# Four graph layers on one core: the relation layer gathers node features with their gates and applies the relation weights per unit of nodes, with no table per relation

## The chip, the core and the metric

The program runs on one core of a Trainium2 chip. The metric is the device time of one execution in microseconds (us), median of the runs. TensorE is called PE below, VectorE DVE, ScalarE ACT, GpSimd POOL, SyncE SP.

## What is computed

There are 6250 nodes with 128 features each and 106250 edges, sorted by destination: 17 per node on average, the node's own loop among them. Four layers follow one another, and each ends in a residual and a layer norm without weights. The third is the one that is changed:

```python
xw = einsum('ni,rio->rno', h, W)              # 8 relations
msg = xw[rel, src] + bias_term[rel]
gate = sigmoid(sum(msg * gw[rel], -1) + gate_bias[rel])
agg = segment_sum(msg * gate[:, None], dst)
out = relu(agg + h @ loop_weight)
```

The first and the fourth layer are attention layers, the second an edge MLP with two layer norms. Every one of them gathers one row per edge from a table of the nodes in HBM, and sums per destination.

## The kernel before, in words

Edges are worked through in 104 groups of 1024, 8 tiles of 128 edges each (`T` = 8, `NG` = 104). Nodes are 49 tiles of 128. They are finished in 13 units of 4 tiles (the last two of 3 and 2), once the groups that hold their edges are summed, so some 8.5 groups lie between one unit and the next. All time is spent in passes, one program per engine and pass, with a barrier of all engines between them: `first_tables`, `gat_pass(0)`, `mlp_pass`, `rel_pass`, `gat_pass(1)`. A check on the drawn edges picks between a fast and a slow path (`pick`, flag `fits`); the profile shows the fast one.

The order of the work is written out by hand. `drive` walks steps: in step n it emits the stages of a group (stage with lag k for group n - k) and then the pieces of units that are due (unit `at` + lag). Each engine runs its list in order and meets the others at semaphores.

`rel_pass` before. POOL issues 8 indirect DMAs per group (L1254, 831 in all), each of which fetches 128 rows of 128 floats from `rel_table`, which has a row for every node and relation, bias and gate already in it (50176 rows). The ring of row buffers is 8 groups deep: gather n waits until group n - 8 is summed. DVE builds the one-hot matrix `hot` of a group in one instruction (L1281, four buffers), PE multiplies rows by it, 8 products of 128 x 128 x 128 into one half-bank (L1411, two buffers `p_sum`), DVE adds the 128 columns to `acc` at the group's base, which it reads into a register first (`window`, L1287). In step n DVE does `one_hot(n)` and then `add(n-1)`, and PE's `add_up(n)` waits for `add(n-2)` only:

```python
pe.wait_ge(s.onehot, n + 1)
pe.wait_ge(s.gathered[n % RING], landed(sh, n))
wait(pe, s.added, n - 1)
```

A unit's `multiply` is 2 products a tile (L1427, L1428), then DVE's `residual` (L1294, L1295 and the moments L691 to L705), ACT's square root and scaling, transposes, the table product of the last layer (L1441) and its evacuation (L1316).

`mlp_pass` before. It gathers rows of 256 floats (L1593), adds the edge product (L1624), takes ACT's squares (L1789), scales and shifts them on DVE (L1630, L1632), gelu on ACT (L1799), sums on PE (L1889). The rows of `rel_table` are made behind the last sum, for all 49 tiles: two PE products of 512 columns a tile (L1954), DVE adds the bias for 1024 columns (L1746) and multiplies half of them by the gate (L1750), ACT the other half (L1855), SP stores 512 KB a tile. The row buffers and the PSUM banks of the groups are used for it, which is why it stands behind them. POOL clears `acc` when the last unit is multiplied (L1615, L1616).

## Time and profile before

| what | value |
|---|---|
| median of 3 runs | 4501.29 us (4498.23 to 4502.14) |
| span of the profiled execution | 5314.6 us, mean granted PE clock 0.674 |
| busy share of the span | PE 59%, DVE 47%, ACT 25%, POOL 60% |
| DMA | 567 MB, mean 107 GB/s |

The profiled execution gives its span only, and no time around it; it is 18% above the median of the runs, which are taken without the profiler. A row of the groups view gives busy time and mean ns of one instruction, then the idle time of the engine ahead of it and who ended it. Register loads, branches, waits and the issuing of DMAs don't count as busy and have no rows. An fp32 product on PE is two MATMUL instructions, so 8 products are 16 rows.

### The profile page before, as it was taken

To read this page: it belongs to the slowest core of one execution; us is meant where nothing else is said; L and a number is where in the kernel's file an instruction comes from. 1 tells how busy PE (TensorE), PEld (TensorE's weight loads), DVE (VectorE), ACT (ScalarE), POOL (GpSimd) and SP (SyncE) were. 2 spreads that over 40 slices of the span, in tenths; PEclk is the share of its full clock that TensorE was granted. 3 is DMA by queue.
4 is the path that set the end of the run, shared out by engine and by line. 5 is a ranking of instruction groups with operands and counts; after the bars stand their busy time and mean duration, and the time that the engine had idled before them with its cause. 6 is when DMAs were issued, how large, how long until landed. Compare 5 with 4: busy or idle time off the path is not lost. (4 is left out here: it accounts for less than half of the span.)

```text
span 5314.6 us, 52198 instructions
## 1 busy us (share of the span) xinstructions
PE 3112.7 (59%) x15416; PEld 2793.1 (53%) x15416; DVE 2515.0 (47%) x5316; ACT 1308.4 (25%) x3470; POOL 3165.2 (60%) x3335
## 2 busy tenths in 40 slices
PE   2666666666377787777871323333332666666666
PEld 2665666566366676666731223323231666666665
DVE  2344444445377878777870111112121454554555
ACT  0010010011267777777760000000000011111111
POOL 5666666663566666666206666666654666666662
PEclk6556556666689888988895566665665565555656
DMA  5444444443444444444241111111112333333331
GB/s 140 128 144 139 151 142 140 151 140 110 138 134 145 147 144 144 143 144 148 81 189 47 48 49 49 50 49 47 52 43 67 97 95 97 99 95 97 98 96 52
DMA packets 284107, 567.22 MB, mean 107 GB/s; under 512 B 108648, under 2 KB 157034, under 8 KB 283802
## 3 DMA queue, kind: packets, MB, share of 16 engines
q0 software_dynamic: 119664, 280.17, 20.3%
q1 hardware_dynamic: 157082, 278.92, 15.4%
q10 hardware_dynamic: 7056, 4.56, 0.3%
q8 instruction: 131, 2.15, 0.2%
q14 instruction: 174, 1.43, 0.1%
HBM read 465.83 MB, written 97.56 MB: 106 GB/s over the span
## 5 line engine op out<-in xcount | busy, mean ns | idle before, releaser
L840 POOL DMA_INDIRECT rows<-gat_table,src_i x1662 | 1568.6, 944 | 861.4 <-issue 464.9
L1593 POOL DMA_INDIRECT rows<-mlp_table,src_i x831 | 789.5, 950 | 527.0 <-issue 303.8
L1254 POOL DMA_INDIRECT rows<-rel_table,rel_i x831 | 783.9, 943 | 494.8 <-issue 343.4
L1129 PE MATMUL p_sum<-rows,hot 128*128 128x133 f32 x3328 | 781.6, 425 | 14.2 <-DVE rows L906 12.5
L1121 PEld LDWEIGHTS p_adc<-adw,hot_t 128*128 128x128 f32 x3328 | 688.1, 314 | 178.0 <-DVE hot_t L880 127.5
L1121 PE MATMUL p_adc<-adw,hot_t 128*128 128x8 f32 x3328 | 678.0, 342 | 147.7 <-DVE hot_t L880 108.4
L1129 PEld LDWEIGHTS p_sum<-rows,hot 128*128 128x128 f32 x3328 | 735.9, 326 | 17.2 <-DVE rows L906 15.6
L1411 PE MATMUL p_sum<-hot,rows 128*128 128x128 f32 x1664 | 324.5, 363 | 715.9 <-DVE hot L1281 365.9
L1411 PEld LDWEIGHTS p_sum<-hot,rows 128*128 128x128 f32 x1664 | 298.6, 272 | 744.3 <-DVE hot L1281 381.2
L1061 ACT COPY sums<-p_sum 128x133 f32<-128x133 f32 x208 | 56.4, 271 | 2211.6 <-DMA rel_index<-rel_i 1902.6
L1889 PE MATMUL p_sum<-hot,rows 128*128 128x128 f32 x3328 | 476.0, 310 | 201.8 <-ACT rows L1799 107.7
L1889 PEld LDWEIGHTS p_sum<-hot,rows 128*128 128x128 f32 x3328 | 461.3, 224 | 236.5 <-ACT rows L1799 123.5
L1136 PE MATMUL p_turn<-ident,sums 128*128 128x128 f32 x208 | 90.7, 436 | 781.1 <-ACT sums L1061 724.7
L906 DVE TENSOR_TENSOR rows<-rows,p_weight 128x1024 f32<-128x1024 f32 x208 | 253.7, 1220 | 610.5 <-ACT p_weight L1056 448.2
L1872 PE MATMUL p_pre<-w1e,eat 128*128 128x256 f32 x1664 | 436.8, 415 | 105.3 <-issue 104.4
L1136 PEld LDWEIGHTS p_turn<-ident,sums 128*128 128x128 f32 x208 | 35.5, 171 | 834.5 <-ACT sums L1061 772.8
L1287 DVE TENSOR_TENSOR acc_t<-acc_t,p_sum 128x128 f32 x104 | 29.8, 286 | 864.3 <-remote 775.9
L1872 PEld LDWEIGHTS p_pre<-w1e,eat 128*128 128x128 f32 x1664 | 337.3, 209 | 172.5 <-issue 123.3
L1789 ACT ACTIVATE junk<-rows 128x256 f32<-128x256 f32 x832 | 335.6, 404 | 294.5 <-DVE rows L1624 179.0
L1624 DVE TENSOR_TENSOR rows<-rows,p_pre 128x1024 f32<-128x1024 f32 x208 | 247.6, 1218 | 281.1 <-PE p_pre L1872 112.2
L1630 DVE SCALAR_TENSOR_TENSOR rows<-rows,stats,p_affine 128x256 f32<-128x256 f32 x832 | 335.1, 475 | 8.3
L886 DVE TENSOR_TENSOR z<-rows,p_adc 128x32 f32<-128x32 f32 x208 | 39.0, 188 | 561.1 <-remote 312.0
(239 smaller groups left out, 3693.9 us busy)
## 6 DMA issues: line engine op xcount, KB each, us to landing
drow<-in_dst_rows SPq DMA_DIRECT2D x208, 512.0 KB
hot_table<-hot SPq DMA_DIRECT2D x104, 512.0 KB
hot<-hot_table SPq DMA_DIRECT2D x104, 512.0 KB
rows<-gat_table,src_i POOLq DMA_INDIRECT x1662
rel_table<-rows SPq DMA_DIRECT2D x49, 512.0 KB, 2.6
eat<-in_edge_t SPq DMA_DIRECT2D x104, 128.0 KB
rows<-mlp_table,src_i POOLq DMA_INDIRECT x831
rows<-rel_table,rel_i POOLq DMA_INDIRECT x831
```

Source lines behind the costliest of these rows:

```text
L840: pool.indirect_dma_start(out=rows[:, n % RING, t, :], out_offset=None, in_=net.gat_table[:, :], in_offset=bass.IndirectOffsetOnAxis(ap=ne ...
L906: nc.vector.tensor_tensor(hr, hr, wt, ALU.mult).then_inc(s.messages, 1)
L1121: end = nc.tensor.matmul(p_adc[k][:, t, 0:2 * H], hot_t[:, k, t * P:(t + 1) * P], adw[:, half, :], start=True, stop=True)
L1129: end = nc.tensor.matmul(p_sum[:, 0:SUMS], hot[:, n % HALF, t, :], rows[:, n % RING, t, 0:SUMS], start=(t == 0), stop=(t == T - 1))
L1254: pool.indirect_dma_start(out=rows[:, n % RING, t, :], out_offset=None, in_=net.rel_table[:, :], in_offset=bass.IndirectOffsetOnAxis(ap=ne ...
L1411: end = nc.tensor.matmul(p_sum[n % 2][:, 0:P], rows[:, n % RING, t, :], hot[:, n % HALF, t, :], start=(t == 0), stop=(t == T - 1))
L1593: pool.indirect_dma_start(out=rows[:, n % RING, t, :], out_offset=None, in_=net.mlp_table[:, :], in_offset=bass.IndirectOffsetOnAxis(ap=ne ...
L1624: nc.vector.tensor_tensor(rows[:, slot, tt, :], rows[:, slot, tt, :], p_pre[half][:, :, :], ALU.add).then_inc(s.pre, 1)
L1630: nc.vector.scalar_tensor_tensor(rows[:, slot, t, :], rows[:, slot, t, :], stats[:, slot, 1, t:t + 1], p_affine[:, 0, :], ALU.mult, ALU.mult)
L1789: nc.scalar.activation(junk[:, t % (T // 2), :], rows[:, slot, t, :], ACT.Square, accum_out=stats[:, slot, 0, t:t + 1])
L1872: end = nc.tensor.matmul(p_pre[half][:, j, :], eat[:, ring, half, :], w1e[:, j, :], start=True, stop=True)
L1889: end = nc.tensor.matmul(p_sum[k][:, b, :], rows[:, n % RING, t, b * F:(b + 1) * F], hot[:, half, t, :], start=(t == 0), stop=(t == T - 1))
```

## The change

The relation layer is turned round: sum first, multiply after. The table `gated_table` has one row per node: 128 features plus one, and 8 gates (`GATED` = 136 floats). `mlp_pass` writes it unit by unit: DVE `lift` adds 1 to the features, PE transposes them and multiplies by `rel_gate` (8 columns), DVE adds the gate bias, ACT takes tanh, DVE turns that into the sigmoid. The bias of a relation is spread over its weights once (`lift_weights`), which the added 1 makes up for. 9 of the 13 units do this between groups, 4 (`late`) behind the last one; the last unit starts 4 steps after the one before it and not 6 (`LAST_APART`). POOL clears most of `acc` ahead of the last unit's product. The index of node and relation, its load of edge types in `first_tables`, and its store are gone.

In `rel_pass` the gathers read `gated_table` with the node's index. A group is cut into 4 pairs of tiles (`PAIRS`), each with 24 nodes x 8 relations = 192 columns (`KEYS`) from its own first destination. Per group DVE picks the edge's gate out of 8 (three small instructions), builds `hot` as 8 instructions of 192 columns (is the key equal, times gate), PE does 8 products with 192 columns into 4 sums, and DVE adds 4 pieces of 192 columns to a ring of 12 node tiles by 8 relations, each at a place that it reads into a register. PE's wait is now for `add(n-1)`, and DVE does `add` ahead of `one_hot`. `multiply` has 9 products a tile, one with the loop weight and 8 with the relation weights on every eighth column of the ring, and `residual` clears 1024 columns a tile. `prepare` works out keys and ring places once, ahead of the first group (some 17 DVE instructions on up to 832 columns). A second flag, `near`, worked out at the start of `gat_pass(0)`, picks the fast path of this pass: every edge of a pair within 24 nodes of its first, and the ring not overrun. The slow path is rewritten too (not shown).

```diff
+PAIRS = T // 2
+SPAN = 24
+KEYS = SPAN * R
+RING_TILES = 12
+GATED = F + R
...
+        self.ring = self.acc[:, :, :].rearrange("p a c -> p (a c)")
...
-        self.rel_table = dram("rel_table", (sh.NP * R, F))
-        self.rel_index = dram("rel_index", (P, sh.NG, T), I32)
+        self.gated_table = dram("gated_table", (sh.NP, GATED))
...
+        rows = s.sb("rows", [P, RING, T, GATED])
+        hot = s.sb("hot", [P, HALF, T, KEYS])
...
-        p_sum = [s.ps(f"p_sum{k}", [P, 512]) for k in range(2)]
-        p_iota = s.ps("p_iota", [P, P])
+        p_sum = [s.ps(f"p_sum{k}", [P, 2, 2 * P]) for k in range(2)]
+        p_keys = s.ps("p_keys", [P, KEYS])
...
-                        out=rows[:, n % RING, t, :], out_offset=None, in_=net.rel_table[:, :],
-                        in_offset=bass.IndirectOffsetOnAxis(ap=net.rel_i[:, n, t:t + 1], axis=0),
+                        out=rows[:, n % RING, t, :], out_offset=None, in_=net.gated_table[:, :],
+                        in_offset=bass.IndirectOffsetOnAxis(ap=net.src_i[:, n, t:t + 1], axis=0),
...
+            def gated(kinds, slot):
+                nc.vector.tensor_tensor(mask[:, :, :], tiled(kinds, T, R), over_tiles(p_keys[:, 0:R], T, R), ALU.is_equal)
+                dve.drain()
+                nc.vector.tensor_tensor(mask[:, :, :], mask[:, :, :], rows[:, slot, :, F:GATED], ALU.mult)
+                dve.drain()
             def one_hot(n):
+                dve.wait_ge(s.gathered[n % RING], landed(sh, n))
+                gated(types[:, n, :], n % RING)
+                nc.vector.tensor_reduce(gate[:, n % 2, :], mask[:, :, :], AX.X, ALU.add)
+                dve.drain()
                 wait(dve, s.summed, n - HALF + 1)
-                nc.vector.tensor_tensor(hot[:, n % HALF, :, :], tiled(net.reld[:, n, :], T, P), over_tiles(p_iota[:, :], T, P), ALU.is_equal).then_inc(s.onehot, 1)
+                for t in range(T):
+                    end = nc.vector.tensor_scalar(hot[:, n % HALF, t, :], p_keys[:, :], key[:, n, t:t + 1], gate[:, n % 2, t:t + 1], ALU.is_equal, ALU.mult)
+                end.then_inc(s.onehot, 1)
 
             def add(n):
-                first = window(dve, net, n)
                 dve.wait_ge(s.summed, n + 1)
-                part = net.acc[:, 0, bass.ds(first, P)]
-                nc.vector.tensor_tensor(part, part, p_sum[n % 2][:, 0:P], ALU.add)
-                dve.drain().then_inc(s.added, 1)
-            def residual(unit):
+                for w in range(PAIRS):
+                    v = n * PAIRS + w
+                    first = dve.value_load(ring_i[0:1, v:v + 1], min_val=0, max_val=MARGIN - R)
+                    part = net.ring[:, bass.ds(first, KEYS)]
+                    nc.vector.tensor_tensor(part, part, p_sum[w // 2][:, w % 2, 0:KEYS], ALU.add)
+                    end = dve.drain()
+                end.then_inc(s.added, 1)
+            def close(unit):
+                for t in range(unit.first, unit.first + unit.tiles):
+                    if t and t % RING_TILES == 0:
+                        nc.vector.tensor_tensor(net.ring[:, 0:KEYS], net.ring[:, 0:KEYS], net.ring[:, MARGIN:MARGIN + KEYS], ALU.add)
+                        dve.drain()
+                        nc.vector.memset(net.ring[:, MARGIN:MARGIN + KEYS], 0.0)
+                dve.drain().then_inc(s.closed, 1)
+            def residual(unit, fast):
 
                 m, tiles = unit.tiles, tiles_of(unit)
                 dve.wait_ge(s.node_product, unit.u + 1)
                 nc.vector.scalar_tensor_tensor(net.x[:, tiles, :], pu[:, 0:m, :], 0.0, net.x[:, tiles, :], ALU.max, ALU.add)
-                nc.vector.memset(net.acc[:, 0, columns(unit)], 0.0)
+                if fast:
+                    for t in range(unit.first, unit.first + m):
+                        nc.vector.memset(net.ring[:, ring_at(t) * R:(ring_at(t) + P) * R], 0.0)
+                else:
+                    nc.vector.memset(net.acc[:, 0, columns(unit)], 0.0)
...
-                drive(sh, [(one_hot, 0), (add, 1)], pieces)
+                drive(sh, [(add, 1), (one_hot, 0)], pieces(True))
...
-                pe.wait_ge(s.gathered[n % RING], landed(sh, n))
-                wait(pe, s.added, n - 1)
+                wait(pe, s.added, n)
                 for t in range(T):
-                    end = nc.tensor.matmul(p_sum[n % 2][:, 0:P], rows[:, n % RING, t, :], hot[:, n % HALF, t, :], start=(t == 0), stop=(t == T - 1))
+                    w = t * PAIRS // T
+                    end = nc.tensor.matmul(p_sum[w // 2][:, w % 2, 0:KEYS], rows[:, n % RING, t, 0:F], hot[:, n % HALF, t, :],
+                                           start=(t % (T // PAIRS) == 0), stop=(t % (T // PAIRS) == T // PAIRS - 1))
...
+                        pe.wait_ge(s.closed, unit.u + 1)
+                    else:
+                        pe.wait_ge(s.added, sh.NG * sh.NT)
+                    pe.wait_ge(s.xt_ready, unit.u + 1)
+                    wait(pe, s.variance, unit.u)
+                split = min(2, unit.tiles)
+                for t in (range(split), range(split, unit.tiles))[part]:
+                    nc.tensor.matmul(pu[:, t, :], xt[:, t, :], lw[:, :], start=True, stop=False)
+                    if fast:
+                        first = ring_at(unit.first + t)
+                        for r in range(R):
+                            end = nc.tensor.matmul(pu[:, t, :], by_relation[:, first:first + P, r], net.rel_w[:, r, :], start=False, stop=(r == R - 1))
...
-                for i in range(unit.tiles):
-                    t = unit.first + i
-                    sp.wait_ge(s.dve_scaled, t + 1)
-                    sp.wait_ge(s.act_scaled, t + 1)
-                    sp.dma_start(table[t:t + 1, :, :].rearrange("t p c -> p (t c)"), tab_of(unit, i).rearrange("p r f -> p (r f)")).then_inc(s.stored[unit.u % TABS], 16)
-            pieces = [(load_unit_weights, WEIGHTS_FIRST), (store_table, OfTable(1))]
+                sp.wait_ge(s.tab_done, unit.u + 1)
+                sp.dma_start(table[:, tiles_of(unit), :], stage[:, unit.u % 2, 0:unit.tiles, :]).then_inc(s.stored[unit.u % 2], 16)
+            pieces = [(load_unit_weights, WEIGHTS_FIRST), (store_table, OfTable(4 + HALF))]
...
-            def evacuate(unit, fast):
-                k = unit.u % 2
+                dve.drain().then_inc(s.outer_factored, 1)
+            def lift(unit):
+                m, k = unit.tiles, unit.u % 2
+                dve.wait_ge(s.normed, unit.u + 1)
+                wait(dve, s.stored[k], 16 * (unit.u // 2))
+                nc.vector.tensor_scalar(stage[:, k, 0:m, 0:F], net.x[:, tiles_of(unit), :], 1.0, None, ALU.add).then_inc(s.lifted, 1)
+            def gate_logits(unit):
+                m = unit.tiles
                 dve.wait_ge(s.gate_product, unit.u + 1)
-                wait(dve, s.gate_ready, unit.u)
-                nc.vector.tensor_tensor(logit[:, 0:unit.tiles, :], p_gate[:, 0:unit.tiles, :], over_tiles(net.rel_gate_bias[:, :], unit.tiles, R), ALU.add).then_inc(s.gate_logits, 1)
-                dve.wait_ge(s.summed, sums_done(fast))
-                wait(dve, s.stored[unit.u % TABS], 16 * kept_before(unit, TABS))
-                for i in range(unit.tiles):
-                    t = unit.first + i
-                    tab = tab_of(unit, i)
-                    dve.wait_ge(s.tab_product, t + 1)
-                    nc.vector.tensor_tensor(tab, p_tab[t % 2], net.rel_b[:, :, :], ALU.add).then_inc(s.tab_read, 1)
-                    dve.drain()
-                    if i == 0:
-                        dve.wait_ge(s.gate_ready, unit.u + 1)
-                    nc.vector.tensor_tensor(tab[:, 0:by_dve, :], tab[:, 0:by_dve, :], tiled(gate[:, k, i, 0:by_dve], by_dve, F), ALU.mult).then_inc(s.dve_scaled, 1)
-            def pieces(fast):
-                return steps + [(lambda unit: evacuate(unit, fast), OfTable(1))]
-            steps = [(copy_w2t, WEIGHTS_FIRST + 2), (fold_gates, WEIGHTS_FIRST + 3), (join, 6), (inner_factors, 8), (node_affine, 9), (residual, 11), (outer_factors, 13)]
+                nc.vector.tensor_tensor(logit[:, 0:m, :], p_gate(unit)[:, 0:m, :], over_tiles(net.rel_gate_bias[:, :], m, R), ALU.add).then_inc(s.gate_logits, 1)
+            def gates(unit):
+                m = unit.tiles
+                dve.wait_ge(s.curved, unit.u + 1)
+                nc.vector.tensor_scalar(stage[:, unit.u % 2, 0:m, F:GATED], curve[:, 0:m, :], 0.5, 0.5, ALU.mult, ALU.add)
+                dve.drain().then_inc(s.tab_done, 1)
+            steps = [(copy_w2t, WEIGHTS_FIRST + 2), (lambda unit: lift_weights(unit, 0), WEIGHTS_FIRST + 4), (lambda unit: lift_weights(unit, 1), WEIGHTS_FIRST + 5),
+                     (fold_gates, WEIGHTS_FIRST + 6), (join, 6), (inner_factors, 8), (node_affine, 9), (residual, 11), (outer_factors, 13),
+                     (lift, NORMED_AT), (gate_logits, OfTable(2)), (gates, OfTable(4))]
```

DVE in the relation pass, one steady step. Names: `combined_1` and `inner_turned_1` are printed for the semaphore `summed`, `stored2_1` for `gathered`; L663 and L1374 load a register; ISA rows are register work. Before:

```order
L1281 TENSOR_TENSOR hot<-reld_all,p_iota 128x1024 [waits combined_1]
L663 TENSOR_LOAD base_i
L663 ISA x2
L1287 ISA [waits combined_1]
L1287 TENSOR_TENSOR acc_t<-acc_t,p_sum_5 128x128
```

In the change:

```order
L1374 TENSOR_LOAD ring_i [waits inner_turned_1]
L1374 ISA x2
L1376 ISA
L1376 TENSOR_TENSOR acc_t<-acc_t,p_sum_5 128x192
L1374 TENSOR_LOAD ring_i
L1374 ISA x2
L1376 ISA
L1376 TENSOR_TENSOR acc_t<-acc_t,p_sum_5 128x192
...
L1354 TENSOR_TENSOR mask<-types,p_keys 128x64 [waits stored2_1]
L1356 TENSOR_TENSOR mask<-mask,rows 128x64
L1363 TENSOR_REDUCE gate<-mask 128x8
L1367 TENSOR_SCALAR hot<-p_keys,key,gate 128x192 [waits inner_turned_1]
L1367 TENSOR_SCALAR hot<-p_keys,key,gate 128x192 x7
```

The register load stood ahead of the wait for the sum and now stands behind it, four times, and everything that PE needs for the next group comes behind that.

PE at a unit of the relation pass, between two groups. Before:

```order
L1427 MATMUL pu_5<-ident,acc_t 128x128 [waits base_spread_1,folded_1]
L1428 MATMUL pu_5<-lw_5,xt_5 128x128
L1427 MATMUL pu_5<-ident,acc_t 128x128
L1428 MATMUL pu_5<-lw_5,xt_5 128x128
L1427 MATMUL pu_5<-ident,acc_t 128x128
L1428 MATMUL pu_5<-lw_5,xt_5 128x128
```

In the change:

```order
L1570 MATMUL pu<-lw,xt 128x128 [waits tab_done_1,product_1,base_ready_1]
L1574 MATMUL pu<-rel_w,acc_t 128x128 x8
L1570 MATMUL pu<-lw,xt 128x128
L1574 MATMUL pu<-rel_w,acc_t 128x128 x8
L1570 MATMUL pu<-lw,xt 128x128
```

Eight products of a unit became 36, in the same place between two groups.

## Rows read from the trace of the kernel before

**Rows 1.** Stages: us from the start, length, busy of each engine, PEclk, DMA share, GB/s

```profile
core 0: us, PE busy (x) PEld busy (x) DVE busy (x) ACT busy (x) POOL busy (x), PEclk, DMA share, GB/s
0.00:51.00 51.00, 23.71 (x159) 22.43 (x159) 23.73 (x76) 8.57 (x14) 11.86 (x8) 0.90 0.65 174
51.00:1260.00 1209.00, 760.66 (x3519) 707.58 (x3519) 539.25 (x1203) 97.26 (x370) 784.04 (x831) 0.60 0.48 141
1260.00:1339.00 79.00, 50.20 (x263) 43.03 (x262) 44.88 (x123) 13.45 (x40) 0.00 (x0) 0.69 0.19 66
1339.00:2576.00 1237.00, 910.99 (x5080) 801.26 (x5080) 909.59 (x1647) 843.82 (x2092) 789.52 (x831) 0.86 0.46 144
2576.00:2646.00 70.00, 57.51 (x343) 52.07 (x343) 56.31 (x114) 48.53 (x113) 0.00 (x0) 0.85 0.12 38
2646.00:2790.00 144.00, 116.42 (x365) 57.51 (x363) 105.13 (x172) 94.17 (x256) 10.80 (x2) 0.92 0.45 180
2790.00:3969.00 1179.00, 368.18 (x1914) 338.63 (x1914) 189.60 (x386) 38.30 (x82) 783.94 (x831) 0.61 0.19 49
3969.00:4025.00 56.00, 24.91 (x143) 22.53 (x142) 21.63 (x72) 9.31 (x21) 0.52 (x2) 0.65 0.07 15
4025.00:5230.00 1205.00, 752.73 (x3397) 705.04 (x3397) 571.73 (x1362) 136.11 (x431) 784.14 (x831) 0.58 0.36 96
5230.00:5314.60 84.60, 47.39 (x238) 42.99 (x237) 53.19 (x164) 18.87 (x51) 0.35 (x1) 0.63 0.07 22
```

**Rows 2.** The timeline of the relation pass: start, us, engine, line, idle before

```profile
2788.93 0.29 DVE L1336 COPY p_iota<-iota_row 128x128 f32<-128x128 f32 x1 [4.92 <-PEq L204]
2790.06 2.35 DVE L1281 TENSOR_TENSOR hot<-reld_all,p_iota 128x1024 f32<-128x1024 f32 x2 [0.83 <-issue]
2791.46 0.95 POOL L1254 DMA_INDIRECT rows<-rel_table,rel_i  x1 [0.30 <-issue]
2792.71 0.94 POOL L1254 DMA_INDIRECT rows<-rel_table,rel_i  x1 [0.30 <-issue]
...
3020.79 6.77 PE L1411 MATMUL p_sum<-hot,rows 128*128 128x128 f32 x32 [4.47 <-issue]
3021.05 0.16 DVE L714 TENSOR_TENSOR work<-scale 128x4 f32<-128x4 f32 x1
3021.30 0.16 DVE L716 SCALAR_TENSOR_TENSOR work<-work 128x4 f32<-128x4 f32 x1
...
3057.68 0.29 DVE L1287 TENSOR_TENSOR acc_t<-acc_t,p_sum 128x128 f32 x1 [2.43 <-PE p_sum L1411]
3058.09 1.22 DVE L1281 TENSOR_TENSOR hot<-reld_all,p_iota 128x1024 f32<-128x1024 f32 x1
```

**Rows 3.** Who waited for whom in the relation pass

```profile
DVE acc_t L1287 <- remote: 764.8, 45, 43.2
POOL rows L1254 <- remote: 150.5, 29, 10.7
```

**Rows 4.** Groups by shape on DVE: relation pass, then the first attention pass, then MLP

```profile
L1287 DVE TENSOR_TENSOR acc_t<-acc_t,p_sum 128x128 f32 x97 | 27.8, 286 | 847.8 <-remote 764.8 <-issue 50.6 <-PE p_sum L1411 32.5
...
L1294 DVE SCALAR_TENSOR_TENSOR x_nodes<-pu,x_nodes 128x512 f32<-128x512 f32 x10 | 6.9, 691 | 28.7 <-remote 28.1
...
L942 DVE MEMSET acc_t<- 128x1024 f32 x10 | 9.1, 912 | 1.6 <-issue 1.6
...
L892 DVE TENSOR_SCALAR z<-z 128x32 f32<-128x32 f32 x98 | 20.2, 206 | 7.9 <-issue 0.4
```

**Rows 5.** Timeline of the MLP pass, DVE: eight instructions of 256 columns, two pointers

```profile
2007.36 3.22 DVE L1630 SCALAR_TENSOR_TENSOR rows<-rows,stats,p_affine 128x256 f32<-128x256 f32 x8
```

**Rows 6.** Groups by shape in the stretch of the table, 2646 to 2790 us

```profile
L1954 PE MATMUL p_pre<-rel_w,hot 128*128 128x512 f32 x196 | 98.1, 647 | 8.8 <-DVE rows L1746 8.8
L1855 ACT ACTIVATE rows<-rows,gate 128x128 f32<-128x128 f32 x196 | 62.6, 390 | 37.3 <-DVE rows L1746 36.9
L1746 DVE TENSOR_TENSOR rows<-p_pre,rel_b 128x1024 f32<-128x1024 f32 x49 | 59.7, 1219 | 10.4 <-PE p_pre L1954 10.4
...
L1750 DVE TENSOR_TENSOR rows<-rows,gate 128x512 f32<-128x512 f32 x49 | 33.9, 692 | 8.9 <-ACT gate L1849 4.7
```

450 lines of the change are left out of this document (275 added, 175 removed).

## The prediction

> **What bounds the kernel now.** I read the stages first [rows 1]. Four stretches of 1179 to 1237 us hold 831 gathers each, 4830 of 5315 us; the other six add up to 484.6 us. In the four, POOL has the same 784 to 790 us of work, while PE ranges from 368 to 911 us and DVE from 190 to 910. What they share is the gather. The timeline shows its pace: one starts each 1.25 us, 0.94 us of work and 0.30 us in which nothing is waited for [rows 2]. 831 of these are 1039 us. The waits then show why the relation pass took 1179 us: POOL stood 151 us on a full ring of row buffers, and DVE waited 765 us in 45 pieces, 17 us each, for something the profile can't name [rows 3], far more than PE's work between them explains. While no gathers run, in the table stretch, DVE shows no such waits [rows 6]. The ring of 8 groups hides most of them.
>
> The profiled execution is 813 us longer than the median of 4501.3. If the 484.6 us outside the gathers cost the same in both, a gather costs (4501.3 - 484.6) / 3324 = 1.208 us in the timed runs, less than the unblocked 1.25 of the profile. So in the timed runs POOL is hardly blocked, and these waits are mostly the profiler's. I sum against the median: engine time is taken over from the rows one to one, the gather at 1.208. The relation pass then has 1004 us of gathers, 9.66 us a group. Against its own time the same sum would be 5315 plus the differences below, and more for the waits named under the rivals.
>
> **What goes.** The table stretch: 144 us in the profile, of which PE's products are 98 us and DVE's two instructions 94 us for 49 tiles [rows 6]. What stays behind the last sum is the chain of the last unit (two tiles) with three late units beside it. For that I take 35 us, an estimate from the 56 us stretch that ends the relation pass with its two last units [rows 1]; with less waiting in a timed run the stretch was 110 to 144 us, so 75 to 109 us go. I take **85 us**. POOL's two clears lay beside it and cost nothing before or after. The edge types, the index and its store were in the first 51 us, beside the node loads; 0 to 3 us, taken as 0, covered by the tables of that stage. The row fetched grows from 512 to 544 bytes with DMA at 0.19 busy: no cost. POOL issues the same 831 gathers.
>
> **What is added outside the relation pass.** DVE gets `lift`, the logits and the gates for 9 units in the MLP pass, some 1 us a unit, and ACT a tanh whose table may have to be loaded. DVE is 74% busy there, 8.7 us a group [rows 1], against 9.66 us of gathers, so little cover is left: **8 us**, bounds 0 and 25. The work for the flag at the start of `gat_pass(0)` is some 8 us on DVE while 8 groups of gathers run ahead, and DVE is 45% busy there: nothing.
>
> **What changes in the relation pass.** Before, DVE and PE had slack: `hot` was four buffers ahead and the sum had two. Now follow the new order. PE's group n needs `hot(n)`; DVE builds that behind `add(n-1)`; that waits for PE's group n-1. Nothing overlaps: a group costs DVE's adds, plus DVE's one-hot, plus PE's products. Piece by piece:
>
> - Adds. Before, one add with its drain took 0.41 us from start to start (57.68 to 58.09) [rows 2]; 64 more columns at one a cycle are 0.07. Each now has a register load in its way, behind the drain of the add before. No row shows a load. The gap of 0.83 us ahead of the first `hot` [rows 2] holds one load and a branch: upper bound 0.83, lower bound 0 (it could run under the add). I take three quarters of that gap, 0.62, since the drain stands between. 4 x (0.41 + 0.07 + 0.62) = **4.4 us**, bounds 1.9 and 5.2.
> - One-hot. Three small instructions with drains: those of 4 columns start 0.25 us apart [rows 2], of 32 columns they take 0.04 more [rows 4], so 0.28 each, 0.84. Then eight of 192 columns with two pointers each and a PSUM source. Nearest are the eight of 256 columns in 3.22 us [rows 5], 0.40 each, less 0.07 for 64 columns: 0.33 each, 2.65. Together **3.5 us**, bounds 2.8 and 3.8.
> - Products. 32 instructions of 128 columns took 6.77 us, 0.212 each [rows 2], at the lower of the two clock levels (1.2 GHz). 16 of 192 columns are 5.1 us there and half at 2.4 GHz. Stretches with PE about half busy or more between gathers show a mean granted clock of 0.58 to 0.61 [rows 1]; 2.55 / 0.6 = **4.25 us**, bounds 2.6 and 5.1.
> - Three hand-overs and the last product's way through: 0.4 us.
>
> The loop is 12.55 us, against 9.66 for the gathers. So the loop becomes the bound: 104 x 12.55 = 1305 us. On top, per unit: PE's 36 products are 72 instructions at 0.177 us (0.6 of the clock), 12.7 us, beside 7.9 us of DVE's adds and one-hot, so 4.8 us show. DVE's residual is 0.69 + 4 x 0.91 [rows 4] and some 1.6 us of moments, 5.9 us beside 4.65 us of PE, 1.3 us. 13 units: 80 us. `prepare` takes DVE some 11 us and its loads 3, beside the first 10 us of gathers: 4 us. The pass is 1389 us in place of 1004, **+385 us**.
>
> A register load has a price in the Trainium skill: DMA: Bandwidth & Descriptors, in the section on latency and other measured facts, gives about 600 ns as its floor. By that the sum would be 8 us lower; no row here shows it. The Trainium skill also speaks against where the keys lie: VectorE: DVE Perf Modes, Why PSUM operands drop a tier, says that an fp32 instruction with a PSUM operand runs at the plain rate, while one with a single SBUF source could run twice as fast. By that the eight instructions would lose 0.1 us each with keys in SBUF, 83 us over the pass; no row of this trace has such an instruction.
>
> **Sum.** 4501 + 385 - 85 + 8 = 4809, forecast **4810 us**.
>
> **Rivals.**
>
> 1. The loop still fits under the gathers. Then only the table's saving shows: 4501 - 85 + 8 = **4424 us**. It decides where the loop falls below 9.6 us, 3 us under my sum. For it: loads that hide (0 and not 0.62) give 2.5 us, full clock 1.7. Against it: both would have to come at once, and the pass before held the clock at 0.61 [rows 1]. Chance 0.09.
> 2. The waits of DVE [rows 3] are not only the profiler's. Before, a ring of 8 groups swallowed them; a loop that is itself the bound has no such cushion, and each wait lengthens it. Of 765 us at most 151 blocked POOL, so some 600 us are added: 4810 + 600 = **5410 us**. It decides as soon as waits of 17 us occur in timed runs. Against it is the 1.208 us. A weaker form of it is why my range reaches further up. Chance 0.08.
> 3. The change doesn't do what it says: the flag `near` falls, and the slow path runs. That has 49 x 8 x 8 products a group at 0.21 us or more, over 60 ms in all. With 17 edges per node 256 edges cover some 15 nodes, against 24 allowed, so 0.01.
> 4. Costs and saving cancel within 9 us: 0.02.
>
> My forecast has 0.80. **Range.** At the low ends together short of rival 1, a loop of 10.6 us and a saving of 105, the time is 4501 + (1102 + 40 - 1004) - 105 + 5 = 4539. At the high ends, a loop of 14.4 with 130 us for units, saving 75: 4501 + 624 - 75 + 10 = 5060, and some waits left. I give 4550 to 5120. Slower than before by over 0.2% (9 us, about what a measurement can tell from no change): forecast, rivals 2 and 3, 0.89; faster 0.09; the same 0.02.
>
> **What would show it.** In the changed kernel's profile POOL's gathers of the relation pass should be interrupted in every group, waiting for PE's last product, and the pass should be much longer than 1179 us. The adds should start 1.1 us apart, the eight one-hot instructions 0.33 us apart, and PE should start each group right behind the last of them, never behind a gather. The stretch between the last MLP gather and the first relation gather should shrink from 214 us to some 110 to 140. I am wrong if gathers run at 1.25 us without waits, if adds come 0.5 us apart, or if DVE's waits of 17 us fill the pass and the time is above 5120.

## The result, and the profile after

The changed kernel takes **4934.8 us** (median of 4 runs, 4932.7 to 4939.2) against 4500.3 (4498.2 to 4502.1) for the kernel before: **1.097 times as long, interval 1.095 to 1.098**, 435 us slower. The forecast was 4810 with a range of 4550 to 5120, so it held in sign and range and came out 125 us short.

The profiled execution of before that stands ahead of the prediction was a disturbed one: its span was 5314.6 us, 813 more than its runs. The same kernel, profiled again beside the experiments, has a span of 4503.3. Stages are therefore compared with that second profile. Here are its stages, in the columns of [rows 1]: the MLP pass, the stretch that makes the table of relations, the relation pass up to its last add, and what lies between that and the first gather of the last layer:

```profile
1126.50:2168.00 1041.50, 855.05 (x5243) 771.77 (x5244) 932.90 (x1701) 862.46 (x2154) 788.39 (x831) 0.93 0.55 173
2168.00:2348.50 180.50, 142.52 (x544) 81.77 (x543) 136.34 (x232) 119.26 (x308) 11.33 (x3) 0.92 0.37 148
2348.50:3392.00 1043.50, 439.23 (x2021) 414.26 (x2022) 204.72 (x417) 41.73 (x90) 783.97 (x831) 0.62 0.22 56
3392.00:3427.00 35.00, 9.26 (x37) 7.28 (x35) 9.67 (x42) 5.88 (x13) 0.48 (x1) 0.55 0.05 13
```

And the same four stretches of the changed kernel:

```profile
1122.00:2166.00 1044.00, 857.48 (x5292) 770.60 (x5293) 924.62 (x1691) 857.81 (x2144) 790.80 (x831) 0.93 0.57 174
2166.00:2256.00 90.00, 50.13 (x307) 44.93 (x305) 64.44 (x163) 56.18 (x118) 11.53 (x5) 0.78 0.09 27
2256.00:3802.00 1546.00, 686.31 (x2656) 660.97 (x2657) 637.83 (x1824) 41.76 (x90) 784.72 (x831) 0.69 0.17 40
3802.00:3855.40 53.40, 21.64 (x88) 19.74 (x87) 14.08 (x47) 5.89 (x13) 0.48 (x1) 0.64 0.04 9
```

POOL works 784 us in the relation pass both times. The pass is 1546.0 us now and was 1043.4, +502.6. The stretch ahead of it is 90.6 and was 181.0, -90.4. Behind the last add it is 53.5 and was 35.0, +18.5. The first stage with the first attention pass gives -4.4, the MLP pass +2.1, all the rest -0.8. That is +427.6, the difference of the two spans (4930.9 and 4503.3). Outside the relation pass and its two neighbours nothing moved.

The waits of the relation pass say who holds up whom. Columns: engine and what it waited for, us in all, times, the longest. These answer to [rows 3]:

```profile
PE p_sum L1549 <- DVE hot L1367: 866.4, 93, 25.8
...
DVE acc_t L1376 <- PE p_sum L1549: 493.2, 90, 5.9
POOL rows L1327 <- PE p_sum L1549: 418.3, 82, 9.1
...
DVE acc_t L1376 <- issue: 274.2, 326, 6.3
```

There are no waits of DVE on something unnamed any more. PE waits for the one-hots, DVE for PE's product, POOL for PE's product, in nearly every group. One group in the timeline, of DVE and PE, shows the circle; it answers to [rows 2]:

```profile
2379.16 0.22 DVE L1354 TENSOR_TENSOR mask<-types,p_keys 128x64 f32<-128x64 f32 x1
2379.46 0.23 DVE L1356 TENSOR_TENSOR mask<-mask,rows 128x64 f32<-128x64 f32 x1
2379.76 0.22 DVE L1363 TENSOR_REDUCE gate<-mask 128x8 f32<-128x64 f32 x1
2380.06 3.17 DVE L1367 TENSOR_SCALAR hot<-p_keys,key,gate 128x192 f32<-128x192 f32 x8
...
2383.29 4.82 PE L1549 MATMUL p_sum<-hot,rows 128*128 128x192 f32 x16 [8.73 <-DVE hot L1367]
...
2388.87 0.35 DVE L1376 TENSOR_TENSOR acc_t<-acc_t,p_sum 128x192 f32 x1 [5.63 <-PE p_sum L1549]
...
2389.99 0.36 DVE L1376 TENSOR_TENSOR acc_t<-acc_t,p_sum 128x192 f32 x1 [0.77 <-issue]
...
2391.12 0.35 DVE L1376 TENSOR_TENSOR acc_t<-acc_t,p_sum 128x192 f32 x1 [0.77 <-issue]
...
2392.25 0.35 DVE L1376 TENSOR_TENSOR acc_t<-acc_t,p_sum 128x192 f32 x1 [0.77 <-issue]
...
2392.72 0.22 DVE L1354 TENSOR_TENSOR mask<-types,p_keys 128x64 f32<-128x64 f32 x1
```

From mask to mask is 13.56 us: 0.90 for the mask and gate, 3.2 for eight one-hots, PE's first product 0.06 behind them, 4.82 of products, 0.76 to the first add, three more adds 1.13 apart, 0.47 to the next mask. In such a group DVE and PE never work at once. The granted clock of PE was 0.50 for the first 4.0 us of these products and 1.00 from 2387.3 us on, when they were nearly done. The 81 cycles away from the units are 13.73 us in the mean. In the 1.13 us from add to add only 0.35 are the add; the idle 0.77 in front of each holds a drain and a register load, which have no rows.

The groups by shape, up to 3370 us, which answer to [rows 4]:

```profile
L1367 DVE TENSOR_SCALAR hot<-p_keys,key,gate 128x192 f32<-128x192 f32 x600 | 238.0, 469 | 6.9 <-issue 1.2
L1376 DVE TENSOR_TENSOR acc_t<-acc_t,p_sum 128x192 f32 x296 | 104.9, 354 | 544.8 <-PE p_sum L1549 351.0 <-issue 193.7
```

### The profile page after: what moved, and what is told of

The parts are those of the page before. It is cut to its first block and busy times, and to the rows that moved or that the text cites. A ratio compares the mean times of both kernels' runs of the same rounds, so it can differ in the third digit from the quotient of the medians.

```text
span 4930.9 us, 56065 instructions
## 1 busy us (share of the span) xinstructions
PE 3180.4 (64%) x15914; PEld 2923.8 (59%) x15914; DVE 2866.6 (58%) x6664; ACT 1243.1 (25%) x3270; POOL 3169.7 (64%) x3336
## 3 DMA queue, kind: packets, MB, share of 16 engines
q1 hardware_dynamic: 156940, 256.65, 15.9%
## 5 line engine op out<-in xcount | busy, mean ns | idle before, releaser
L1327 POOL DMA_INDIRECT rows<-gated_table,src_i x831 | 784.8, 944 | 672.5 <-PE p_sum L1549 418.3
L1549 PE MATMUL p_sum<-hot,rows 128*128 128x192 f32 x1664 | 486.1, 474 | 866.4 <-DVE hot L1367 866.4
L1549 PEld LDWEIGHTS p_sum<-hot,rows 128*128 128x128 f32 x1664 | 456.8, 299 | 891.3 <-DVE hot L1367 891.3
L1170 PEld LDWEIGHTS p_adc<-adw,hot_t 128*128 128x128 f32 x3328 | 632.4, 292 | 564.1 <-DVE hot_t L905 562.0
L1178 PE MATMUL p_sum<-rows,hot 128*128 128x133 f32 x3328 | 745.3, 411 | 3.1 <-DVE rows L931 2.9
L1376 DVE TENSOR_TENSOR acc_t<-acc_t,p_sum 128x192 f32 x416 | 147.4, 354 | 767.4 <-PE p_sum L1549 493.2
L2052 PE MATMUL p_sum<-hot,rows 128*128 128x128 f32 x3328 | 449.6, 300 | 174.8 <-ACT rows L1971 174.8
L2052 PEld LDWEIGHTS p_sum<-hot,rows 128*128 128x128 f32 x3328 | 433.7, 214 | 208.7 <-ACT rows L1971 207.7
L911 DVE TENSOR_TENSOR z<-rows,p_adc 128x32 f32<-128x32 f32 x208 | 39.1, 188 | 745.6 <-DMA rows<-gat_table,src_i 723.2
L2035 PE MATMUL p_pre<-w1e,eat 128*128 128x256 f32 x1664 | 385.5, 385 | 23.6 <-DVEq L1943 21.4
L1367 DVE TENSOR_SCALAR hot<-p_keys,key,gate 128x192 f32<-128x192 f32 x832 | 330.1, 469 | 9.2 <-issue 1.2
L905 DVE TENSOR_TENSOR hot_t<-drow,p_adc 128x1024 f32<-128x1024 int32 x208 | 253.9, 1221 | 16.0 <-issue 0.4
```

The lines of the kernel that those rows point to most:

```text
L905: nc.vector.tensor_tensor(hot_t[:, k, :], drow[:, half, :], p_base.broadcast_to([P, GE]), ALU.is_equal).then_inc(s.turned_onehot, 1)
L1170: end = nc.tensor.matmul(p_adc[k][:, t, 0:2 * H], hot_t[:, k, t * P:(t + 1) * P], adw[:, half, :], start=True, stop=True)
L1178: end = nc.tensor.matmul(p_sum[:, 0:SUMS], hot[:, n % HALF, t, :], rows[:, n % RING, t, 0:SUMS], start=(t == 0), stop=(t == T - 1))
L1327: pool.indirect_dma_start(out=rows[:, n % RING, t, :], out_offset=None, in_=net.gated_table[:, :], in_offset=bass.IndirectOffsetOnAxis(ap= ...
L1367: end = nc.vector.tensor_scalar(hot[:, n % HALF, t, :], p_keys[:, :], key[:, n, t:t + 1], gate[:, n % 2, t:t + 1], ALU.is_equal, ALU.mult)
L1549: end = nc.tensor.matmul(p_sum[w // 2][:, w % 2, 0:KEYS], rows[:, n % RING, t, 0:F], hot[:, n % HALF, t, :], start=(t % (T // PAIRS) == 0) ...
```

## The experiments

Each is run beside the kernel before on the same chip, with 4 runs of its own (experiment 1 with one). Ratios are to that kernel. All edits are to the changed kernel, unless said otherwise.

**1. The kernel before, unchanged.**

> The kernel before, unchanged, to get a second trace of it. Theory (the 17 us waits of DVE were of that one profiled execution and not of the timed runs): the span is about 4497 us, near the median, gathers start 1.25 us apart in all four stretches with no waits on a full ring, and the six other stretches hold about 345 us (4500 less 3324 gathers at 1.25) and not 485. Rival (the waits belong to the kernel): the span is again near 5300 with DVE waiting 765 us in the relation pass.

4505.0 us, span 4503.3. The 831 gathers of the relation pass lay in 1036.0 us, those of the other three layers in 1036.3, 1040.9 and 1039.0: one per 1.248 to 1.254 us, the 1.25 of [rows 2]. The 17 us waits of [rows 3] are absent, so they belong to that one execution. But the six other stretches add up to 4503.3 - 4152.2 = 351 us and not 484.6. The step "if the 484.6 us cost the same in both, a gather costs 1.208 us" was wrong: the disturbance had lengthened those stretches as well.

**2. One-hots of group n ahead of the adds of group n - 1.**

```diff
-                drive(sh, [(add, 1), (one_hot, 0)], pieces(True))
+                drive(sh, [(one_hot, 0), (add, 1)], pieces(True))
```

> The changed kernel with one_hot(n) ahead of add(n-1) on DVE, nothing else. Theory (the loop of adds, one-hot and products is serial and bounds the relation pass at 13.6 us a group): one-hot, 4.1 us, now runs beside PE's products, the loop is 4.6 + 1.1 + 3.8 = 9.5 us, just under the 10.0 us of the gathers, which become the bound again: about 4480 us (4460 to 4540). Rival (PE or DVE is short of throughput, or the wider rows slow the gathers): no change, 4935 us.

4618.3 us, ratio 1.0265 (1.0248 to 1.0282): 317 us gone through one exchanged pair, yet 138 more than expected. The timeline of PE and DVE over one cycle:

```profile
2313.19 0.35 DVE L1376 TENSOR_TENSOR acc_t<-acc_t,p_sum 128x192 f32 x1 [0.77 <-issue]
...
2313.72 5.46 PE L1549 MATMUL p_sum<-hot,rows 128*128 128x192 f32 x16 [5.04 <-DVEq L1377]
...
2314.65 0.22 DVE L1354 TENSOR_TENSOR mask<-types,p_keys 128x64 f32<-128x64 f32 x1 [1.11 <-DMA rows<-gated_table,src_i]
...
2315.55 3.17 DVE L1367 TENSOR_SCALAR hot<-p_keys,key,gate 128x192 f32<-128x192 f32 x8
...
2319.94 0.35 DVE L1376 TENSOR_TENSOR acc_t<-acc_t,p_sum 128x192 f32 x1 [1.22 <-PE p_sum L1549]
...
2323.32 0.35 DVE L1376 TENSOR_TENSOR acc_t<-acc_t,p_sum 128x192 f32 x1 [0.77 <-issue]
...
2323.84 5.46 PE L1549 MATMUL p_sum<-hot,rows 128*128 128x192 f32 x16 [4.67 <-DVEq L1377]
```

The one-hots now wait for their gather (the 1.11 us of idle time ahead of the mask ends with a DMA) and lie beside PE's products. What is left is the loop of products and adds through the single `p_sum`: 5.46 + 0.76 + 3.38 + 0.52 = 10.12 us. That is 0.13 more than the 9.99 of eight gathers. So hardly anything is left over to take up a unit: the two cycles around one were 21.2 and 15.4 us, 16 more than two normal ones, only a few cycles behind it were shorter (8.9 to 9.9 us), and the pass is 1232 us up to its last add. I had expected a loop short of the gathers by some tenths, and the units in its slack.

**3. The four register loads ahead of the wait for PE.**

```diff
                 dve.wait_ge(s.summed, n + 1)
...
+                firsts = [dve.value_load(ring_i[0:1, n * PAIRS + w:n * PAIRS + w + 1], min_val=0, max_val=MARGIN - R) for w in range(PAIRS)]
...
-                    first = dve.value_load(ring_i[0:1, v:v + 1], min_val=0, max_val=MARGIN - R)
-                    part = net.ring[:, bass.ds(first, KEYS)]
+                    part = net.ring[:, bass.ds(firsts[w], KEYS)]
```

> The changed kernel with the four register loads of add ahead of its wait for the sum, into four registers. Theory (each load is exposed, 0.58 to 0.62 us): they run beside PE's products, 2.4 us less a group, 104 groups: 4935 - 250 = 4685 us. Rival (the drains and not the loads make the 1.13 us between adds): 4920 to 4935 us.

4731.7 us, ratio 1.0515 (1.0498 to 1.0533), 203 us less. The adds came 0.51 us apart in place of 1.13, and the first one 0.47 us behind the start of PE's last product in place of 1.09: **0.62 us a load, as the prediction had it** from three quarters of the 0.83 us gap. The mean cycle away from the units fell from 13.73 to 11.23 us, the full 2.5, or 260 us over the pass. Some 55 came back at the units, whose two cycles cost 14.6 us more than two normal ones and not 9.4. That a shorter loop covers less of PE's work for them would explain it; no run isolates it.

**4. Keys in SBUF.** `p_keys` goes, and the one-hots (and the first mask) read `keys` in its place; the values are the same.

```diff
-                    end = nc.vector.tensor_scalar(hot[:, n % HALF, t, :], p_keys[:, :], key[:, n, t:t + 1], gate[:, n % 2, t:t + 1], ALU.is_equal, ALU.mult)
+                    end = nc.vector.tensor_scalar(hot[:, n % HALF, t, :], keys[:, :], key[:, n, t:t + 1], gate[:, n % 2, t:t + 1], ALU.is_equal, ALU.mult)
```

> The changed kernel with the row of keys read from SBUF and not from PSUM. By the rule of the Trainium skill (VectorE: DVE Perf Modes, Why PSUM operands drop a tier) the eight one-hot instructions run at twice the rate, 0.285 and not 0.385 us each, 0.8 us a group: 4935 - 83 = 4850 us. Rival 1 (the source makes no difference): 4935. Rival 2 (DVE at the double rate holds up the issue of gathers): gathers more than 1.25 us apart, but they have slack in this kernel, so the time is between the two.

4913.0 us, ratio 1.0917 (1.0899 to 1.0936), 22 us less and not 83. The groups of the same stretch as above:

```profile
L1366 DVE TENSOR_SCALAR hot<-keys,key,gate 128x192 f32<-128x192 f32 x608 | 195.2, 391 | 6.4 <-issue 0.4
...
L1547 PE MATMUL p_sum<-hot,rows 128*128 128x192 f32 x1216 | 381.5, 501 | 595.8 <-DVE hot L1366 595.8
```

```profile
L1549 PE MATMUL p_sum<-hot,rows 128*128 128x192 f32 x1198 | 348.9, 473 | 631.3 <-DVE hot L1367 631.3
```

One-hots went from 469 to 391 ns of mean. The eight of a group took 3.17 us in the changed kernel, always, and 2.43 to 2.7 here. Two groups:

```profile
2379.26 2.43 DVE L1366 TENSOR_SCALAR hot<-keys,key,gate 128x192 f32<-128x192 f32 x8
...
2392.73 2.69 DVE L1366 TENSOR_SCALAR hot<-keys,key,gate 128x192 f32<-128x192 f32 x8
```

Taken one by one, 576 of the 728 steps from one one-hot to the next were 0.29 us, where the changed kernel has 0.387. The other 152 were 0.40, and 148 of them began 0.45 to 0.65 us behind the start of one of POOL's gathers. In all that is 0.6 us a group, some 64 us over the pass. By the rule in the Trainium skill (VectorE: DVE Perf Modes, Why PSUM operands drop a tier) the 192 columns could have gone twice as fast, 0.1 us less; the trace agrees for these four in five. Why the others miss it was not tried beyond this coincidence. But PE's products (the row of L1549 is the changed kernel's own) rose from 473 to 501 ns of mean: away from the units a group's took 5.27 us in the mean, where the changed kernel had 4.91. So nearly 0.4 of the 0.6 us were given back by PE's slower products, and the mean cycle fell by 0.27 us only.

**5. Edits 2 and 3 together.**

> The changed kernel with both edits: one-hots of group n before the adds of group n-1, and the four register loads before the wait for PE. Theory (the relation pass is set by the loop PE products, DVE adds, PE products, and by POOL's gathers under it): the loop is 4.93 us of products at the low clock, 0.66 to the first add, 1.53 us of adds, 0.5 back to PE = 7.6 us, under the 10.0 us of eight gathers; each unit still costs 10 to 16 us but 2.4 us a group over 8 groups is taken up again. So the gathers run at 1.25 us with few waits: 4501 less the 90 us of the shorter start plus 10 to 30 us of units at the end = 4430 us, range 4405 to 4475, faster than the kernel before. Rival (each edit only saves what it saved alone, 317 and 203 us, with no bound under them): 4935 - 520 = 4415, with gathers still waiting each group. Rival (units bound the pass: 13 times 16 us not taken up): 4560.

**4446.4 us, ratio 0.9877 (0.9861 to 0.9894): 1.2% faster than the kernel before.** The relation pass against POOL, in the waits of its gathers:

```profile
POOL rows L1327 <- issue: 278.7, 831, 25.8
```

No wait for PE is left, and the 831 gathers lie in 1036.8 us. The loop of products and adds is some 7.6 us at the low clock (5.46 of products, 0.14 to the first add, 3 x 0.51, 0.5 back to PE; an estimate from these pieces), 2.4 under eight gathers, and the backlog of a unit (cycles of 20.5 and 13.7 us) is taken up again in four cycles of 6.3 to 7.2 us. The two edits saved 317 and 203 us alone and 488 together, where the gathers stop them.

**6. Keys in SBUF, sums in four banks, DVE's order as it was.**

```diff
-        p_sum = [s.ps(f"p_sum{k}", [P, 2, 2 * P]) for k in range(2)]
+        p_sum = [s.ps(f"p_sum{k}", [P, 2, 2 * P]) for k in range(4)]
...
-                wait(pe, s.added, n)
+                wait(pe, s.added, n - 1)
```

> Keys in SBUF as in the run at 4913 us, and p_sum in four banks in place of two, so that PE need not wait for the adds of the group before but of the one before that; DVE's order stays adds first. Theory (the order on DVE is what makes the loop serial, not the single set of sums): PE's group n+1 still waits for one-hots that stand behind the adds of group n, so no change: 4913 us, range 4900 to 4920, and PE still starts right behind the last one-hot. Rival (the single p_sum is what ties PE to DVE): the loop falls by the adds, 3.4 us or more a group, to about 4560.

4911.5 us against 4913.0 for edit 4: no change. The second set of sums, which the kernel before had, is worth nothing while DVE's list puts the adds first.

**8. The same with one-hots ahead of the adds** (edits 6 and 2).

> Keys in SBUF, sums in four banks, and one-hots of group n before the adds of group n-1 (register loads left between the adds). Theory (what binds at 4618 us is the loop PE, adds, PE of 10.13 us, through the single set of sums): with two sets PE's group n+1 runs beside DVE's adds of group n; DVE has 3.38 + 0.9 + 2.25 + some 1.3 of wake-ups and waits, 8 us a group, under 10.0, so the gathers set the pace: 4440 us, range 4410 to 4480. Rival (DVE's serial chain of one-hots, wait, adds is the loop, with PE's products in it): the gain over 4618 is only the 0.45 us a group of the shorter one-hots, about 4570 or no change.

4441.3 us, ratio 0.9866 (0.9850 to 0.9882), gathers in 1037.2 us. Against run 2 it has a second set of sums and the keys in SBUF; the keys alone are worth at most the 0.6 us a group of edit 4. This removes the bound of run 2 in another way: PE runs group n + 1 beside DVE's adds of group n, the cycle is 9.99 us, and the register loads cost nothing although they are all still there. The exchange is what is needed; either one of the loads and the second set of sums then does the rest.

**7 and 9. Dummy products in PE's idle time,** 24 and then 38 of 128 columns, ahead of each group's wait, into a spare bank.

```diff
+                if n:
+                    for _ in range(FILL):
+                        nc.tensor.matmul(p_fill[:, 0:F], net.ident[:, :], net.rel_w[:, 0, :], start=True, stop=True)
                 pe.wait_ge(s.onehot, n + 1)
```

> The changed kernel with 24 dummy products of 128 columns into a spare bank of PSUM ahead of each group's wait, in PE's idle time of 9 us a group. They are 5.1 us at the lower clock and 2.6 at the higher, so they end before the one-hots are there. Theory (the products take 4.45 us because PE's idle time takes the clock down, and they are on the loop): with the clock held, 16 products take about 2.5 us in place of 4.45, a group 11.7 us, 4935 - 200 = 4735 us, range 4700 to 4800; the granted clock of the pass rises from 0.69 towards 0.9. Rival (the clock does not follow this idle time): 4935 within 10, products still 4.4 us. Rival (more work takes the clock down): up to 5000, products 4.9 us.

> The changed kernel with 38 dummy products a group in place of 24. With 24 the clock of the pass rose from 0.69 to 0.90, yet PE still stood 3.7 us idle ahead of each group and most products ran 4.2 us; only some ran 2.54. Theory (the idle time just ahead of the products decides their clock): 38 dummies fill 8.7 us of the 9.3 us between the last product and the next one-hots, the products take 2.5 us in nearly every group, the cycle is 11.6 us and the kernel 4935 - 190 = 4745 us, range 4710 to 4800. Rival (the products run at the lower clock after any wait): 4880 as with 24. Rival (the dummies run over into the loop, at the lower clock): above 4935.

4879.8 us with 24 (ratio 1.0841, 1.0822 to 1.0859), 4797.7 with 38 (1.0649, 1.0632 to 1.0667): 55 and 137 us less for work that nobody needs, where 200 and 190 had been expected. Two cycles with 24, and two with 38, on PE:

```profile
2344.06 4.48 PE L1554 MATMUL p_sum<-hot,rows 128*128 128x192 f32 x16 [3.38 <-DVE hot L1369]
2348.33 5.63 PE L1549 MATMUL p_fill<-rel_w,ident 128*128 128x128 f32 x48
2357.28 2.87 PE L1554 MATMUL p_sum<-hot,rows 128*128 128x192 f32 x16 [3.32 <-DVE hot L1369]
2359.98 5.52 PE L1549 MATMUL p_fill<-rel_w,ident 128*128 128x128 f32 x48
```

```profile
2338.99 2.87 PE L1554 MATMUL p_sum<-hot,rows 128*128 128x192 f32 x16 [0.27 <-DVE hot L1369]
2341.70 8.65 PE L1549 MATMUL p_fill<-rel_w,ident 128*128 128x128 f32 x76
2350.59 2.87 PE L1554 MATMUL p_sum<-hot,rows 128*128 128x192 f32 x16 [0.25 <-DVE hot L1369]
```

With 24, 2.1 to 3.8 us of idle time stayed ahead of the products. 64 of the 104 groups took 4.4 us or more, 27 took 2.87 or a little less, and the granted clock of 2260 to 3370 us was 0.90. With 38, 0.7 us or less stayed; from the second group on the products away from the units took 2.87 or a little less, the cycle was 11.8 us in the mean, and the granted clock was 0.99, against 0.69 without dummies. So **PE's clock is a term of this loop, 2.0 us a group**, and PE's idle time in it takes it away. Which idle time counts is not shown: the dummies fill the gap just ahead of the products and the group's whole idle time at once, and with 24 of them the same 3.3 to 3.4 us of waiting stood ahead of slow and of fast groups (both rows above). The whole gain of 200 us did not come since the dummies stand in the way of the units: the cycle of one rose from 20.8 to 27.3 us.

**10. One relation in place of eight in a unit's products** (seven products a tile are left out, and with them seven relations).

```diff
-                        for r in range(R):
-                            end = nc.tensor.matmul(pu[:, t, :], by_relation[:, first:first + P, r], net.rel_w[:, r, :], start=False, stop=(r == R - 1))
+                        for r in range(1):
+                            end = nc.tensor.matmul(pu[:, t, :], by_relation[:, first:first + P, r], net.rel_w[:, r, :], start=False, stop=True)
```

> The changed kernel with each unit's products cut from nine to two per tile (seven of the eight relations are left out of the sum). Prices the units: their products are 36 per unit, some 12 to 16 us of PE with 10 us or so showing on the loop, and 10 us each for the two last units behind the last add. Theory (the units cost the pass 9.6 us each by PE's products): about 28 fewer products, so the 21 us cycle falls to 15 and the stretch behind the last add from 53 to 38 us: 4935 - 11 x 7 - 15 = 4843 us, range 4825 to 4865. Rival (DVE's 6 us of residual and moments, and the waits for them, set the units' cost): 4935 - 15 - 11 x 2 = 4900.

4846.4 us, ratio 1.0761 (1.0743 to 1.0779), 88 us less. The first cycle of a unit fell from 20.8 to 13.6, the second stayed at 15.9, and the stretch behind the last add fell from 53.5 to 39.1. PE's products are most of a unit's price. The 2.3 us of the second cycle stay nearly whole (1.9), as they would if DVE's residual and moments make them.

**12. Neighbouring columns of the ring as weights** (other numbers enter the sums; the products are as many and as large).

```diff
-by_relation[:, first:first + P, r]
+net.ring[:, first * R + r * P:first * R + (r + 1) * P]
```

> The changed kernel with the units' products reading 128 neighbouring columns of the ring instead of one column in eight (other numbers enter these sums; the count and shape of the instructions are the same). In the run with 38 dummy products PE's granted clock was 0.99, the dummies went at 0.114 us each, yet the units' products still took 0.248 us each, and their weight loads 334 ns against 192. Theory (loading weights from every eighth column sets this rate, whatever the clock): with neighbouring columns the 72 instructions of a unit take 8 to 10 us in place of 16.1, the first cycle of a unit falls from 20.8 towards 14 us, and the kernel is about 80 us faster: 4855, range 4835 to 4880. Rival (the accumulation of nine products in one place, or the clock, sets the rate): 4935 within 10, and the products still 0.248 us.

4851.9 us, ratio 1.0777 (1.0759 to 1.0795), 83 us less. A tile's eight relation products on PE in the changed kernel, in the run with 38 dummies, and here:

```profile
2446.83 3.97 PE L1574 MATMUL pu<-rel_w,acc_t 128*128 128x128 f32 x16
```

```profile
2431.97 3.97 PE L1579 MATMUL pu<-rel_w,acc_t 128*128 128x128 f32 x16
```

```profile
2449.17 1.95 PE L1574 MATMUL pu<-rel_w,acc_t 128*128 128x128 f32 x16
```

3.97 us with every eighth column and 1.95 with neighbouring ones. The granted clock over these tiles was 1.00 in all three runs: the 0.69 of the changed kernel is a mean of the pass, and while PE works through a unit it has full speed. So the run with dummies says nothing about the clock here. One tile does: the first one of the last unit, behind the last add, ran wholly at the lower level, a granted clock of 0.50. In the changed kernel, and here:

```profile
3823.39 4.01 PE L1574 MATMUL pu<-rel_w,acc_t 128*128 128x128 f32 x16
```

```profile
3746.58 3.62 PE L1574 MATMUL pu<-rel_w,acc_t 128*128 128x128 f32 x16
```

With the stride 4.01 us at the lower level and 3.97 at the higher; without it 3.62 and 1.95. The stride costs a tenth at the lower clock and doubles the time at the higher one. The weight loads of the pass, by form, of the changed kernel and of this one:

```profile
L1574 PEld LDWEIGHTS pu<-rel_w,acc_t 128*128 128x128 f32 x512 | 124.6, 334 | 0.0
```

```profile
L1574 PEld LDWEIGHTS pu<-rel_w,acc_t 128*128 128x128 f32 x512 | 59.8, 192 | 0.0
```

334 against 192 ns. With the stride it is the weights' read that sets the rate, not PE's clock. The 83 us are nearly all of the 88 of edit 10: at 8.2 us a unit's products fit beside DVE's adds and one-hots, and the first cycle of a unit is 13.6 us again.

**11. The fastest parts together, and a unit's clearing moved behind its moments** (edits 2, 3, 4, 6).

```diff
-                        nc.vector.memset(net.ring[:, ring_at(t) * R:(ring_at(t) + P) * R], 0.0)
...
                 dve.drain().then_inc(s.variance, 1)
+                if fast:
+                    for t in range(unit.first, unit.first + m):
+                        nc.vector.memset(net.ring[:, ring_at(t) * R:(ring_at(t) + P) * R], 0.0)
```

> One-hots first, register loads before the wait, sums in four banks, keys in SBUF, and each unit's clearing of the ring moved behind its moments. Theory (with either of the two edits beside the new order the gathers bound the pass at 1037 us, so both together give nothing more; only the stretch behind the last add, 53 us, can shrink, by 3 and 2 us of clearing of the two last units): 4441 - 5 = 4436 us, range 4430 to 4441. Rival (something of the loop still shows under the gathers): 10 us or more below 4441.

4446.3 us, ratio 0.9870 (0.9854 to 0.9887): the same as the runs of 5 and 8. With the gathers as the bound the other parts give nothing, as expected. The 5 us did not come either (the stretch behind the last add was 56.0 us, and 53.1 in run 8). DVE in that stretch:

```profile
3346.82 0.17 DVE L722 RECIPROCAL work<-work 128x2 f32<-128x2 f32 x1
3347.34 0.91 DVE L1399 MEMSET acc_t<- 128x1024 f32 x1 [0.36 <-issue]
3348.42 0.91 DVE L1399 MEMSET acc_t<- 128x1024 f32 x1 [0.16 <-issue]
3349.41 0.16 DVE L731 TENSOR_TENSOR work<-scale 128x2 f32<-128x2 f32 x1
```

ACT's square root ran from 3347.04 to 3347.24, before the first clearing had begun, and what goes on from it (L731) stands behind both clearings. So the clearing ahead of the root and the clearing behind it stand in the same chain. To leave it, it would have to stand behind the scaling; that wasn't tried.

## Why the prediction was right, and where its sizes were off

**The mechanism** was the one forecast: DVE's adds, its one-hots and PE's products in a circle, 104 times, with nothing beside one another, so that the loop takes the gathers' place as the bound. The waits show it, and run 2, which only lets the one-hots pass the adds, takes 317 us back. The signs named ahead came true: gathers interrupted in each group, adds 1.13 us apart (1.1 said), PE's start right behind the last one-hot. The stretch ahead of the pass shrank to 90.6 us, from 181.0 and not from 214, so the "110 to 140" missed, though the saving did not.

**What goes: 85 us, measured 90.4.** Both ends had been taken from a disturbed profile, with an argument about the difference; run 1 gives it directly.

**Outside the pass: +8, measured +2.1** in the MLP pass (-3.1 with the other stages). The gates and tables of nine units add next to nothing there; the lower bound was the better value.

**The gathers: 1.208 us, measured 1.249.** The pass before was 1043 us up to its last add and not 1004. It made the change look 39 us dearer than it is.

**The loop: 12.55 us, measured 13.73 in the mean,** 123 us over the pass. By the group shown (13.56):
- Adds with their loads 4.4, measured 3.85 + 0.62 = 4.47. Right, and so was the unseen register load; its three quarters of a gap were a guess with a reason, and that they met it to a hundredth was luck. The figure of about 600 ns in the Trainium skill (DMA: Bandwidth & Descriptors, latency and other measured facts) agrees as well.
- One-hots 3.5, measured 0.90 + 8 x 0.385 = 3.98. The step that failed is "0.40 each, less 0.07 for 64 columns": the fewer columns saved 0.015 us, not 0.07. The row it came from [rows 5] has another operation with another operand; which of the two made the difference was not run.
- Products 4.25, measured 4.82 in the group shown. The clock of 0.6 had been read from stretches where PE is half busy, and used as a mean speed. But a group's products are a burst behind 8.7 us of waiting and run mostly at the lower level (5.46 us in run 2 is all of it at that level). Runs 7 and 9 show that PE's idle time is the cause.
- Hand-overs 0.4, measured 0.29.

**The units: 80 us, measured some 103 in the pass and 18.5 behind it.** With 13.73 x 104 = 1428 us of loop and 15 us to the first mask, 1546 leaves 103 us: 9.4 for each of the 11 units that lie before the last add, against 6.1. The step that failed is "72 instructions at 0.177 us (0.6 of the clock), 12.7 us", and it failed twice. The clock was at 1.00 over a unit's products and not at 0.6, which without a stride makes 8.2 us of them (run 12). And the 64 relation products among them take 0.25 us each at either clock (run 12), so that the 72 took 16.1 us. The two errors go against each other, and it is luck that 12.7 lies as near as it does. The Trainium skill has the rule that was missed: SBUF — State Buffer, under Door 1: The DMA port swizzle, says that fp32 is strided for free over up to four elements, and that each access on a new line pays a penalty. Here the step is eight, and the trace agrees, with 0.248 against 0.122 us at the full clock (run 12). It gives no price, but it would have kept these 64 from being priced by a row without a stride.

In sum: 4809, +123 and +23 for the loop and the units in the pass, +11 for its first group (15 in place of 4), -39 for the gathers, +18.5 behind the last add, -5 and -11 for the stretch ahead and the rest, is 4930; the profiled execution took 4930.9. So the 125 us are a net figure: the loop, the units and the start of the pass were 175 us too low, and 55 us of other terms, too high, hid part of that.

**The rivals.** Rival 1, that the loop fits under the gathers (4424 us), is wrong for this kernel, but runs 5, 8 and 11 are just that case: 4441 to 4446. The 17 to 22 us above its price are the two last units behind the last add. Rival 2, that the 17 us waits are real in timed runs, fell with run 1. Rival 3, the slow path, didn't occur.

## What to carry over

Before you turn a product and a sum round, write down each engine's list for one group and follow the circle: here the order of two calls on DVE is worth 317 us, four register loads in the wrong place 203, and with both put right the same change is 1.2% faster than before and not 9.7% slower. Where PE waits in each turn of a circle, price its products at the low clock, and the work of a unit, over which the granted clock was 1.00 here, at the full one. Where an operand is a strided view, price it from a row with that stride or not at all; and take a pace from a profile only when its span agrees with the runs.

## What had not been expected of the hardware

- Weights loaded from every eighth fp32 column: 0.248 us an instruction at the full clock and 0.251 at the lower level; from neighbouring columns 0.122 and 0.226.
- 38 useless products a group made the kernel 137 us faster, by PE's clock alone (4.91 to 2.85 us in the mean for 16 instructions of 192 columns).
- A register load between two drained adds on DVE costs 0.62 us, all of it on the chain; the same load ahead of a wait costs nothing that shows.
- One-hots with their keys in SBUF started 0.29 us apart in place of 0.387, but 0.40 where one began 0.45 to 0.65 us behind the start of a gather of POOL (148 of the 152 slow ones in run 4).
- A shorter wait of PE did not raise its clock: in run 4 the one-hots were 0.6 us shorter and the products nearly 0.4 us longer. Why is open.
